# Step-size terms of two channel blocks summed by TensorE instead of GpSimd, and three more input products on GpSimd

## The reference, cut to what matters

```python
xp = einsum('bld,ed->ble', x, x_proj_w)              # 64 + 16 + 16 columns
delta = softplus(einsum('blr,dr->bld', xp[..., :64], dt_proj_w) + dt_proj_b)
deltaA = exp(einsum('bld,dn->bldn', delta, -exp(A_log)))
deltaB_u = einsum('bld,bln,bld->bldn', delta, Bm, x)  # Bm: 16 columns of xp
h = deltaA[t] * h + deltaB_u[t]                       # over the 1024 positions
y[t] = einsum('bdn,bn->bd', h, Cm[t])                 # Cm: 16 columns of xp
out = y + x * D
```

## Time and profile before

| What | Value |
|---|---|
| Median of 3 runs | 4588.45 us (4587.21 to 4588.93) |
| Profiled execution, its own time | 4593.33 us |
| Its span | 4591.5 us |
| DVE busy in the span | 3897.8 us (85%) |
| POOL busy | 3507.2 us (76%) |
| ACT busy | 2757.9 us (60%) |
| PE busy | 2737.3 us (60%) |
| Mean granted clock of PE | 0.659 of full speed |

### The profile page before, as it was taken

One profiled execution on the slowest core, in us unless ns is written; L12 is line 12 of the kernel. 1 busy time (PEld: TensorE's weight loads), 2 busy tenths in 40 slices (PEclk: granted clock), 3 DMA queues, 4 the chain that ended last, 5 costly groups with the idle time before them and its releaser, 6 DMA issues. The chain is left out here.

```text
span 4591.5 us, 57205 instructions
## 1 busy us (share of the span) xinstructions
PE 2737.3 (60%) x15526; PEld 1027.7 (22%) x15526; DVE 3897.8 (85%) x3322; ACT 2757.9 (60%) x4103; POOL 3507.2 (76%) x1780
## 2 busy tenths in 40 slices
PE   3556454645464645455554645464643289999997
PEld 1111111211111111111111211111211145555553
DVE  3999999999999999999999999999998645555552
ACT  5667777776767677766677777677664222222221
POOL 3999999999999999999999999999997100000000
PEclk7555565656565656555565556565655599999998
DMA  4454546363645455454545463636452300000000
GB/s 104 97 132 118 142 111 160 88 165 90 166 95 149 112 138 139 111 137 113 133 118 150 103 163 84 166 84 170 94 133 74 147 10 24 18 18 18 18 19 7
DMA packets 198208, 472.72 MB, mean 103 GB/s; under 512 B 60688, under 2 KB 61200, under 8 KB 197088
## 3 DMA queue, kind: packets, MB, share of 16 engines
q1 hardware_dynamic: 177136, 452.11, 38.8%
q0 software_dynamic: 20736, 16.88, 1.4%
HBM read 126.83 MB, written 73.43 MB: 44 GB/s over the span
## 5 line engine op out<-in xcount | busy, mean ns | idle before, releaser
L881 POOL TENSOR_TENSOR ch<-hid,cmat 128x1024 f32<-128x1024 f32 x1024 | 2388.0, 2356 | 56.9 <-DVE hid L735 39.0
L735 DVE TENSOR_TENSOR_SCAN hid<-decay,inp 128x1024 f32<-128x1024 f32 x1024 | 2291.9, 2278 | 33.4 <-ACT decay L602 32.4
L399 PE MATMUL ps_y<-ch,nsum 128*32 128x256 f32 x8192 | 998.3, 592 | 883.2 <-POOL ch L881 880.8
L602 ACT ACTIVATE decay<-delr,a_neg 128x1024 f32<-128x1024 f32 x1024 | 1138.9, 1112 | 610.0 <-DVE hid L735 593.6
L724 DVE TENSOR_TENSOR inp<-dx,bmat 128x1024 f32<-128x1024 f32 x848 | 978.2, 1215 | 63.0 <-ACT dx L610 63.0
L399 PEld LDWEIGHTS ps_y<-ch,nsum 128*32 128x32 f32 x8192 | 261.2, 146 | 1593.4 <-POOL ch L881 1346.9
L394 PE MATMUL ps_y<-xhT,dskip 128*32 128x256 f32 x2048 | 270.7, 621 | 436.0 <-DVE xr L745 436.0
L846 POOL TENSOR_TENSOR inp<-dxr,bmat 128x1024 f32<-128x1024 f32 x176 | 415.4, 2360 | 0.0
L1134 POOL DMA_INDIRECT out_rows<-row,idx_out x16 | 41.1, 2571 | 401.3 <-issue 220.2
L408 PE MATMUL ps_y<-ident,ysb 128*128 128x128 f32 x512 | 160.7, 412 | 295.2 <-ACT ysb L617 275.4
L610 ACT ACTIVATE dx<-dxr 128x1024 f32<-128x1024 f32 x256 | 259.2, 1012 | 3.0 <-DMA dxr<-dxT 3.0
(11 more groups left out here) (165 smaller groups left out, 3951.0 us busy)
## 6 DMA issues: line engine op xcount, KB each, us to landing
dxr<-dxT SPq DMA_DIRECT2D x1024, 128.0 KB, 2.4
delr<-delT SPq DMA_DIRECT2D x1024, 128.0 KB, 2.4
xr<-in_x SPq DMA_DIRECT2D x32, 1024.0 KB, 6.3
bmat<-b_and_c SPq DMA_DIRECT2D x256, 128.0 KB, 3.3
cmat<-b_and_c SPq DMA_DIRECT2D x256, 128.0 KB, 2.9
x_rows<-xr SPq DMA_DIRECT2D x16, 2048.0 KB, 7.7
out_rows<-xr SPq DMA_DIRECT2D x32, 1024.0 KB, 4.3
w<-in_w SPq DMA_DIRECT2D x2, 4096.0 KB, 23.9
```

The lines of the kernel that those rows point to most:

```text
L399: last = pe.matmul(ps_y[q * CH:(q + 1) * CH, 0:2 * P], nsum[:], ch[:, g, q * 2 * P:(q + 1) * 2 * P], start=False, stop=(g == GROUPS - 1))
L602: nc.scalar.activation(decay[:, g % 2, :], delr[:, c % 2, :], ACT.Exp, scale=a_neg[:, i:i + 1])\
L735: nc.vector.tensor_tensor_scan(hid[:, g, :], decay[:, g % 2, :], inp[:, g, :], 0.0, ALU.mult, ALU.add).then_inc(hid_ready, 1)
L881: nc.gpsimd.tensor_tensor(ch[:, g, :], hid[:, g, :], cmat[:, g, :], ALU.mult).then_inc(ch_ready, 1)
```

## The change

Blocks 0 and 1 stay as they were. For blocks 2 and 3:

- The work is cut in four half blocks, each with its own four places in the table `HALVES`: `step_size` on PE, `terms` on ACT, `add_terms` on PE, `copy_step` on ACT.
- `terms` makes all four terms of 512 positions in six instructions, into `dxT`, `delT` and two new buffers `eh` and `uh` of 512 columns.
- `add_terms` multiplies the four by the identity, summing in `aux` (four products of 128 x 512, fp32). `copy_step` copies the sum into `delT`.
- POOL loses the three additions of each of these blocks and keeps the product with x (`delta_x`).
- `OWN_AT` gains chunks 2, 7 and 15: POOL makes 14 of the 16 tile-3 inputs of a sequence, not 11, and DVE 50 inputs, not 53.
- `SUMS1`, `SUMS2`, `MAKE_OUT` and `FINISH2` are moved by a place or more. The ring for GpSimd's DMA descriptors goes from 8192 to 4096 bytes of each partition.

```diff
-Z = (12, 13, 15)
-Z3 = 4
+Z = (12, 13)
-         (0, 2): (0, 2, 0), (1, 2): (0, 2, 1), (2, 0): (0, 2, 2), (3, 0): (0, 2, 3),
-         (5, 2): (0, 3, 0), (6, 0): (0, 3, 1), (6, 2): (0, 3, 2), (7, 1): (0, 3, 3)}
+         (2, 1): (0, 2, 3), (7, 0): (0, 3, 3)}
+HALVES = {(2, 0): ((14, 0), (14, 3), (15, 0), (15, 3)), (2, 1): ((0, 0), (0, 3), (1, 0), (1, 3)),
+          (3, 0): ((3, 3), (4, 1), (4, 2), (5, 0)), (3, 1): ((5, 0), (5, 2), (5, 3), (6, 2))}
-OWN_AT = (1, 3, 4, 5, 6, 8, 9, 10, 11, 12, 13)
+OWN_AT = (1, 2, 3, 4, 5, 6, 7, 8, 9, 10, 11, 12, 13, 15)
...
+            def add_terms(b, k, h):
+                aux_free(b, ("s", k, h))
+                pe.wait_ge(terms_act, (b * 4 + 2 * (k - 2) + h) * HACT + HACT)
+                half = slice(h * HALF, (h + 1) * HALF)
+                pe.matmul(aux[:], ident[:], dxT[:, k, half], start=True, stop=False)
+                for term in (eh, uh):
+                    pe.matmul(aux[:], ident[:], term[:], start=False, stop=False)
+                pe.matmul(aux[:], ident[:], delT[:, k, half], start=False, stop=True).then_inc(aux_full, 1)
...
+            def terms(b, k, h):
...
+                aux_filled(b, ("z", k, h))
+                nc.scalar.activation(eh[:], aux[:], ACT.Abs, bias=dtb[:, k:k + 1]).then_inc(terms_act, 1)
+                nc.scalar.activation(dxT[:, k, half], aux[:], ACT.Relu, bias=dtb[:, k:k + 1])\
+                    .then_inc(terms_act, 1)
+                act.wait_ge(terms_act, n + 1)
+                nc.scalar.activation(eh[:], eh[:], ACT.Exp, scale=-1.0).then_inc(terms_act, 1)
+                act.wait_ge(terms_act, n + 3)
+                nc.scalar.activation(uh[:], eh[:], ACT.Identity, bias=1.0).then_inc(terms_act, 1)
+                nc.scalar.activation(delT[:, k, half], eh[:], ACT.Ln, bias=1.0).then_inc(terms_act, 1)
+                act.wait_ge(terms_act, n + 4)
+                nc.scalar.activation(uh[:], uh[:], ACT.Identity, scale=-1.0, bias=1.0).then_inc(aux_emptied, 1)
+
+            def copy_step(b, k, h):
+                aux_filled(b, ("s", k, h))
+                nc.scalar.activation(delT[:, k, h * HALF:(h + 1) * HALF], aux[:], ACT.Copy).then_inc(aux_emptied, 1)
...
                 else:
-                    pool.wait_ge(delta_step, n + 3)
-                    i, j = xhat_slot(k, par)
-                    nc.gpsimd.tensor_tensor(dxT[:, k, :], delT[:, k, :], xhT[:, i, j, :], ALU.mult)\
-                        .then_inc(dx_made[k], 1)
+                    pool.wait_ge(aux_emptied, b * NUSE + USE[("s", k, 1)] + 1)
+                    delta_x(b, par, k)
...
-    nc = bacc.Bacc("TRN2", target_bir_lowering=False, num_devices=1, dynamic_dma_scratch_size=8192)
+    nc = bacc.Bacc("TRN2", target_bir_lowering=False, num_devices=1, dynamic_dma_scratch_size=4096)
```

More of the change, by code:

```diff
@@ L57 @@
 FINISH1 = (7, 0)
-FINISH2 = (2, 1)
+FINISH2 = (2, 3)
 OWN = GROUPS - 1
-OWN_AT = (1, 3, 4, 5, 6, 8, 9, 10, 11, 12, 13)
+OWN_AT = (1, 2, 3, 4, 5, 6, 7, 8, 9, 10, 11, 12, 13, 15)
 ROUTED = (4, 2)
 STORE_LOAD = (3, 4)
-USES = [("xhat", t) for t in range(TC)] + [("proj", 0), ("proj", 1)] + [("z", k, h) for k in range(KD) for h in range(2)]
+USES = [("xhat", t) for t in range(TC)] + [("proj", 0), ("proj", 1)] + [("z", k, h) for k in range(2) for h in range(2)] \
+    + [(stage, k, h) for k in (2, 3) for h in range(2) for stage in "zs"]
 USE = {key: u for u, key in enumerate(USES)}
@@ L74 @@
 ZACT = 6
+HACT = 5
 def xhat_slot(k, par):
@@ L415, in _ @@
                 project(0, 0, h)
-            for k in range(3):
+            for k in range(2):
                 for h in range(2):
                     step_size(0, k, h)
+            step_size(0, 2, 0)
+            add_terms(0, 2, 0)
             pe.wait_ge(dskip_ready, KD)
@@ L429, in body @@
                         sum_states(b, par, c, g)
-                        for h, at in ((0, (Z3 - 1, 3)), (1, (Z3, 1))):
-                            if (c, g) == at:
-                                step_size(b, 3, h)
                         for h, at in ((0, (-1, 3)), (1, (0, 0))):
-                            for k in range(3):
+                            for k in range(2):
                                 if (c, g) == (Z[k] + at[0], at[1]) and not final:
                                     step_size(b + 1, k, h)
+                        for k, h in HALVES:
+                            ahead = int((k, h) == (2, 0))
+                            if ahead and final:
+                                continue
+                            if HALVES[k, h][0] == (c, g):
+                                step_size(b + ahead, k, h)
+                            if HALVES[k, h][2] == (c, g):
+                                add_terms(b + ahead, k, h)
                         if final:
@@ L525, in exp_log @@
                 nc.scalar.activation(tu[:], tu[:], ACT.Identity, scale=-1.0, bias=1.0).then_inc(z_act, 1)
+            def terms(b, k, h):
+                if has(b, 1) and h == 0:
+                    for s in dx_rep + del_rep:
+                        act.wait_ge(s, (b * (CHUNKS // 2) - CHUNKS // 2 + 2 * k + 2) * 16 * NT)
+                half = slice(h * HALF, (h + 1) * HALF)
+                n = (b * 4 + 2 * (k - 2) + h) * HACT
+                aux_filled(b, ("z", k, h))
[12 more added lines that the diff above has]
+                nc.scalar.activation(delT[:, k, h * HALF:(h + 1) * HALF], aux[:], ACT.Copy).then_inc(aux_emptied, 1)
             def copy_rw(b, emptied):
@@ L636, in _ @@
                 copy_proj(0, h)
-            for k in range(3):
-                if k == 2:
-                    copy_dx(0, 0)
-                    for g in range(2):
-                        exp_decay(0, 0, g)
+            for k in range(2):
                 for h in range(2):
@@ L645, in _ @@
                 exp_log(0, k)
+            copy_dx(0, 0)
+            for g in range(2):
+                exp_decay(0, 0, g)
+            terms(0, 2, 0)
+            copy_step(0, 2, 0)
             def beside(b, par, c, place):
                 at = (c, place)
-                if c == Z3 and place == 1:
-                    z_half(b, 3, 0)
-                if c == Z3 and place == 3:
-                    z_half(b, 3, 1)
-                    exp_log(b, 3)
+                for k, h in HALVES:
+                    ahead = int((k, h) == (2, 0))
+                    if ahead and is_last(b):
+                        continue
+                    if HALVES[k, h][1] == at:
+                        terms(b + ahead, k, h)
+                    if HALVES[k, h][3] == at:
+                        copy_step(b + ahead, k, h)
                 if has(b, 1):
```

30 lines of the change are left out of this document (20 added, 10 removed).

## The result

The changed kernel takes 4673.94 us (median of 4 runs, 4671.59 to 4679.39), the kernel before in the same comparison 4588.32 us: a ratio of 1.0184, 95% interval 1.0171 to 1.0197. It is 86 us slower; 4646 was predicted, with a range of 4565 to 4715. The profiled execution took 4675.43 us, 82.1 more than that of before.

A forecast was written before the change was run, and what follows sets the result against it. DVE was taken as the bound, at work some 212 of 216.8 us a sequence. Terms summed to +3.9 us a sequence, +55 over fourteen, +57 with the ends: 4650 on the profiled execution, 4646 us predicted, range 4565 to 4715.

The forecast's parts named there:

- DVE's waits for `decay`: Sign: they grow from 1.8 to 7 us or more of a sequence, mostly ahead of scans (6, 2) and (2, 2).
- What comes off: Three inputs leave DVE, -3.4 us of a sequence; old waits, such as that ahead of scan (5, 2), go, -2.0.
- Chunk 6: ACT waits for z; decay (6, 1) is 0.8 us late and (6, 2), behind eight sums, 3.8: +4.6 of a sequence.
- Chunk 2: ACT waits for PE's identity products, 5.4 us for four; decay (2, 2) comes 2.5 us late.
- rival B: No change: PE runs the new products at the higher clock, chunk 2 loses nothing; 4584 us, chance 0.17.
- rival C: Slower still: all identity products at the lower clock, seven microseconds for eight; 4720 us, chance 0.14.
- Chunk 1: ACT's decays, sums and terms take 10.9 us against DVE's 10.3; decay (1, 2) comes 0.6 us late.
- Chunks 14 to 0: POOL's extra input for (15, 3) delays `add_y` of chunk 15; new waits of 3.7 us replace old ones: +1.6.
- Ahead of the first of the ACT rows and behind the last: First sequence about +2 us, last about -1, and +1.4 once for eight products ahead of the first scan.
- The smaller descriptor ring: Loads might wait for one another, between nothing and 37 us once; taken as nothing.
- Rival A: Faster: ACT isn't late, getting its pieces done while DVE makes its inputs; 4531 us, chance 0.17.
- POOL's new slack: POOL does 88 products, not 91: 7 us of slack, no gain by itself as DVE's list is then longer.

The follow-up runs named there:

- e9: Changed kernel with only the layer-norm sums moved away from between decays (6, 1) and (6, 2), and the wait for a half of x as in e1: 4628.48 us.
- e1: Changed kernel with chunks 4 to 6 rearranged on ACT: sums spread from chunk 4, second half of block 3 later, wait only for the half of x read: 4597.51 us.
- e2: Changed kernel with only chunks 0 to 2 rearranged on ACT: sums moved, second copy_step of block 2 at the start of chunk 2: 4621.77 us.
- e5: Changed kernel with one identity product in place of four, three of the four terms left out of the step size: 4632.1 us.
- e12: Changed kernel with the input of (15, 3) alone back on DVE; (2, 3) and (7, 3) stay on POOL: 4638.4 us.
- e8: e4 with the inputs of (2, 3), (7, 3) and (15, 3) back on DVE: 4534.44 us.
- e10: e4 with the inputs of (2, 3) and (15, 3) back on DVE, (7, 3) on POOL: 4516.4 us.
- e11: e4 with only the input of (15, 3) back on DVE, (7, 3) and (2, 3) on POOL: 4503.35 us.
- e6: Changed kernel with the inputs of (2, 3), (7, 3) and (15, 3) back on DVE: 4650.64 us.
- e4: Changed kernel with the edits of e1, e2 and e3 together: 4533.44 us.
- e3: Changed kernel with POOL's second and third additions for block 1 moved behind tiles (15, 0) and (0, 1): 4652.67 us.

## Why the prediction was right, and where its sizes were off

The direction and the mechanism were right, and so were the places, except inside the turn; the size was 28 us too small. DVE's waits for `decay` grew to 143.7 / 14 = 10.3 us of a sequence, where 7 or more were said; the period of 222.45 is just above the 220 to 222. Step by step, in us of a sequence:

- **What comes off.** DVE's inputs were priced at -3.4 and its work shrank by 3.2. The old waits were priced at -2.0; those ahead of (5, 2) and at `add_y` of chunks 1 and 7 were 1.03 + 0.84 + 0.17, and 0.03 are left.
- **Chunk 6**, predicted +4.6, measured 4.55. From `add_y` of chunk 4 on, z began 2.3, `terms` 4.4 and decay (6, 1) 7.8 us later, each as predicted. The half-width instructions, estimated at 0.56, took 0.61 to 0.63 with starts 0.52 to 0.67 apart; `terms` took the 3.4 us of the sum. e9 shows the half that is the sums'; that of z is shown by the 3.19 us of ACT's wait and by e1, where `terms` stands behind decay (6, 1) and scan (6, 1) doesn't wait.
- **Chunk 2**, predicted +2.5, measured 2.49; e2 and e5 show both of its causes. The products took 4.3 to 5.9 us, median 5.5 (4.8 in the rows above), between rival B's and rival C's reading of the clock and near the 5.4 of the sum: in all sixteen sequences they started at the lower level and went over to the higher within the four.
- **Chunk 1**, predicted +0.6, measured 1.39. In eight of the fourteen sequences ACT doesn't wait there at all, and scan (1, 2) waits 1.58 to 1.67 us. ACT's pieces from decay (1, 0) on take the 10.9 us of the working, but they begin 0.9 to 1.3 us after `add_y` of chunk 15, behind the copy of dx, which the working left out. The sequence ahead of the one above, first ACT, then DVE:

```profile
1864.58 1.02 ACT L659 ACTIVATE dx<-dxr 128x1024 f32<-128x1024 f32 x1
1865.53 1.11 ACT L651 ACTIVATE decay<-delr,a_neg 128x1024 f32<-128x1024 f32 x1
```

```profile
1864.19 0.40 DVE L797 TENSOR_TENSOR xr<-xr,ps_y 128x256 f32<-128x256 f32 x1
...
1876.56 2.29 DVE L787 TENSOR_TENSOR_SCAN hid<-decay,inp 128x1024 f32<-128x1024 f32 x1 [1.67 <-ACT decay L651]
```

In the other six ACT begins earlier and waits for z as in chunk 6, 0.20 to 1.02 us, and the scan waits 0.6 to 1.4.

- **Chunks 14 to 0**, predicted +1.6 (3.7 of new waits for 2.1 of old), measured 4.65 for 2.23, +2.4. This term was too small, and its path was in part another. The working went by the last `ch`, which would hold up `add_y` of chunk 15, and let the old wait at `add_y` of chunk 14 go. That wait stayed, 1.22 us after 1.42; `add_y` of chunk 15 waits 0.53; and the largest piece, 1.78 us, stands ahead of scan (15, 3), which waits for POOL's input itself. The working has no term for that wait; e12, which gives this input back to DVE, has neither the 1.22 nor the 1.78. Chunk 0 adds 0.89, in every second sequence for the most part (last section). That the sum came as near as it did is in part luck.
- **Ahead of the first of the ACT rows and behind the last**, predicted +2.4 us in all, measured 330.74 - 323.68 = +7.1 and, from the last row to the end of the span, -3.7: +3.4. The first stretch goes on into chunk 2 of the second sequence, so that it holds a whole turn. The smaller descriptor ring, which no run took back by itself, was rightly priced at nothing: the sixteen loads of the earlier trace rows are issued within 19 us in both kernels.

Chunk 1 and the turn, 0.8 us each, give nearly all of the 1.7 us by which the period was missed, and that is 24 of the 28 us.

Rival A (ACT isn't late) and rival B (PE at the higher clock, nothing lost in chunk 2) are out by the waits at their places. Rival B's premise held in chunk 4, where the four products took 3.7 to 4.0 us in fourteen of sixteen sequences, and not at the places that it had to save. Rival C's premise held nowhere: in all sequences and places the last pair ran at the higher clock, and the longest four took 6.3 us.

One step of the prediction had the wrong reason. It called POOL's new slack "no gain by itself" and all three inputs a gain of 3.4, against which the waits stood as a separate debt. e8, e10, e11 and e12 show that it is one account for each input: (7, 3) pays in full, (2, 3) pays where ACT is in time (where it isn't, the wait ahead of scan (2, 2) is 1.06 us in e6 and 2.28 in e12), and (15, 3) takes its 1.1 off DVE and brings 3.4 to 3.8 of waits (e4 against e11, the changed kernel against e12), 2.5 us of a sequence lost. It stands in POOL's list ahead of the last four `ch` of a sequence; that this order is the reason is argued, as no run put it at another place in the list.

## What to carry to other kernels

Work moved from a full engine to one with room on the average pays or costs by its place: lay the piece into the receiver's list where it will stand, and look who waits for what is queued behind it. An instruction that waits for another engine, with independent work and then a due result behind it in the same list, costs the wait and the work; with both pieces put elsewhere the 4.6 us of chunk 6 fell to 0.15. A change that came out slower is mended late place by late place before it is dropped: with four tables, one wait and one input put right this one is 87 us faster than the kernel before, not 86 us slower.

## What the runs showed of the hardware

- In the changed kernel the first scan behind the turn of the loop, whose pass holds two sequences, waits for nothing that the profile shows: 1.18 us at 2080.76 ("issue"), 0.98 to 1.65 in the six passes, two of them labelled with POOL's `ch`. It isn't the turn of the loop alone: where DVE makes the input of (15, 3) (before, e6, e8, e10, e11, e12) the same scan doesn't wait, and in e3 and e4, where that input comes in time, it waits 0.26 to 0.62. So the loss goes with that late input; what passes in it stays open.
- A wait named after one engine can belong to another. The 1.78 us ahead of (15, 3) are labelled `decay` in twelve sequences and POOL's input in two; e6 and e12, in which DVE makes that input, have no wait there.
- Within the four identity products of chunk 1 PE's pairs went from 2.08 to 1.02 us, and the granted clock from 0.50 to 1.00, without a pause between them; ahead of the first pair PE had worked for 1.9 us after 1.8 us of waiting for `add_y`.
